# The middle low part of the convolution operands made on GpSimd instead of VectorE, in a fused decoder kernel on one Trainium2 core

## What is computed

```python
x = _layernorm(x + _L0_attn_ref(x, ...), axis=-1)      # 32 heads of 16, softmax attention, output projection wo
x = _layernorm(x + _L0_xattn_ref(x, ctx_1024, ...))    # width-2 causal convolution, gates, cell
x = _layernorm(x + _L0_ffn_ref(x, ...), axis=-1)       # x quantized to integers, ternary weight, bias
```

```python
conv = lax.conv_general_dilated(xp, weight, window_strides=(1,), padding='VALID', ...)
out = uss + conv + bias[None, :, None]
it, ot, gt, ft = jnp.split(out, 4, axis=1)
it, ot, gt, ft = (sigmoid(it), sigmoid(ot), jnp.tanh(gt), sigmoid(ft))
ct = ft * z0c + it * gt
ht = ot * jnp.tanh(ct)
```

## Time and profile before

| | |
|---|---|
| runs | 2153.88, 2157.04, 2160.73 us |
| profiled execution, its own time | 2158.94 us |
| span in the profile, first to last instruction | 2156.9 us |
| mean granted TensorE clock | 0.978 |
| PE busy | 2084.8 us, 97% |
| DVE busy | 1663.5 us, 77% |
| ACT busy | 1313.6 us, 61% |
| POOL busy | 492.8 us, 23% |
| pair 0: projection, convolution | from about 1701, from 1754.75 us |
| pair 1: projection, convolution | from about 1906, from about 1976 us |
| last convolution matmul, end | 2122, 2154.4 us |

### The profile page before, as it was taken

The page is one execution under the profiler, slowest core; times in us unless marked ns, Lnnn a source line. Parts: engine busy times, 40 slices in busy tenths (PEclk is TensorE's granted clock), DMA queues, the critical chain, the costliest instruction groups (busy, mean ns, idle before and its releaser), DMA issues. The chain is left out here.

```text
span 2156.9 us, 39825 instructions
## 1 busy us (share of the span) xinstructions
PE 2084.8 (97%) x11264; PEld 1174.6 (54%) x11264; DVE 1663.5 (77%) x1729; ACT 1313.6 (61%) x2429; POOL 492.8 (23%) x972
## 2 busy tenths in 40 slices
PE   9999999999999999999999999999999899988996
PEld 4788775444444444444444444444444477756773
DVE  4333356888999999999989999998998367885786
ACT  0112113778888888888888888888887533443344
POOL 0000000121212212121221212122121452564244
PEclk9999998999999999999999999999999999998997
DMA  4456645456475565665665564655657567744672
GB/s 161 137 156 157 179 127 98 80 117 135 101 135 130 101 139 112 112 138 97 132 137 101 126 136 101 135 128 103 138 110 207 166 251 302 281 172 137 234 259 79
DMA packets 205965, 315.24 MB, mean 146 GB/s; under 512 B 105168, under 2 KB 105168, under 8 KB 193616
## 3 DMA queue, kind: packets, MB, share of 16 engines
q1 hardware_dynamic: 205904, 314.47, 57.9%
HBM read 211.06 MB, written 101.19 MB: 145 GB/s over the span
## 5 line engine op out<-in xcount | busy, mean ns | idle before, releaser
L233 DVE TENSOR_REDUCE neg_max<-psum 128x1 f32<-128x1024 f32 x1024 | 1205.9, 1219 | 139.8 <-PE psum L226 139.7
L612 ACT ACTIVATE probs<-psum 128x512 f32<-128x512 f32 x2048 | 1065.3, 606 | 281.3 <-PE psum L539 277.0
L539 PE MATMUL psum<-q_op,k_op 50*128 50x512 f32 x2048 | 753.7, 452 | 8.1 <-POOLq L683 3.3
L539 PEld LDWEIGHTS psum<-q_op,k_op 50*128 50x128 f32 x2048 | 354.8, 192 | 586.5 <-ACT probs L612 566.3
L226 PE MATMUL psum<-k_op,q_op 48*128 48x512 f32 x2048 | 623.0, 480 | 0.8 <-DVE neg_max L233 0.8
L548 PE MATMUL psum<-probs,v_op 128*32 128x512 f32 x4096 | 549.8, 609 | 5.7 <-ACT probs L612 2.9
L226 PEld LDWEIGHTS psum<-k_op,q_op 48*128 48x128 f32 x2048 | 390.5, 315 | 20.7 <-issue 4.4
L191 PE MATMUL psum<-x_wino,conv_w 128*128 128x512 f32 x1152 | 275.2, 395 | 0.7 <-DMA conv_w<-conv_w_parts_dram 0.7
L191 PEld LDWEIGHTS psum<-x_wino,conv_w 128*128 128x128 f32 x1152 | 214.6, 188 | 46.7 <-issue 1.1
L244 POOL CAST neg_max_parts<-neg_max 128x8 fp32r<-128x8 f32 x128 | 24.5, 191 | 918.8 <-DVE neg_max L233 918.8
L548 PEld LDWEIGHTS psum<-probs,v_op 128*32 128x32 f32 x4096 | 82.6, 108 | 137.3 <-ACT probs L612 69.3
(11 more groups left out here) (104 smaller groups left out, 1665.5 us busy)
## 6 DMA issues: line engine op xcount, KB each, us to landing
q_op<-qk_parts_dram SPq DMA_DIRECT2D x384, 128.0 KB, 4.1
conv_w<-conv_w_parts_dram SPq DMA_DIRECT2D x32, 1536.0 KB, 6.7
qk_parts_dram<-qk_parts SPq DMA_DIRECT2D x128, 256.0 KB, 3.2
k_op<-qk_parts_dram SPq DMA_DIRECT2D x384, 64.0 KB, 4.1
conv_w_parts_dram<-conv_w_parts SPq DMA_DIRECT2D x16, 1536.0 KB, 6.1
attended_dram<-out SPq DMA_DIRECT2D x64, 256.0 KB, 2.2
attended_parts_dram<-o_parts SPq DMA_DIRECT2D x128, 128.0 KB, 2.3
gates<-in_ctx_dram SPq DMA_DIRECT2D x32, 512.0 KB, 7.6
```

The costliest lines, as they stand in the source:

```text
L233: nc.vector.tensor_reduce(ops["max"][b][:, t:t + 1], mem["pair"][t % 2][:], AX_X, ALU.max, negate=True).then_inc(ops["maxed"], 1)
L539: nc.tensor.matmul(score_bank(i, n, j, last), kop[i][r, j // 2, n // 2 * P:(n // 2 + 1) * P], qop[i][r, j // 2, j % 2 * HALF:(j % 2 + 1) * ...
L612: nc.scalar.activation(probs[n % DEEP][:, j, :], score_bank(k, n, j, last), ACT.Exp, scale=SCALE).then_inc(exp_done, 1)
```

## The change

`low_parts` on VectorE no longer makes the middle low part. A new function of GpSimd, `middle_low`, makes it at the same step of the stage (for the tile of step i - 2), behind `inv_std` of step i and ahead of `last_term` of step i - 1. It waits for the same count of `wx_hi` as VectorE did and counts a new semaphore, `wx_mid`. TensorE waits for `wx_mid` beside `wx_made` in slot 0. The short description that goes with the change also names FFN tiles 7 to 12, brought forward into the last four convolution slots of each pair; the diff, which is whole here, touches no FFN tile and none of the tables.

```diff
@@ -899,6 +899,7 @@
         wx_made = sem("x_wino_made")
+        wx_mid = sem("x_wino_mid_made")
         c_in = [sem(f"c_in{g}") for g in range(4)]
@@ -1102,6 +1103,13 @@
+                def middle_low(p, w):
+
+                    bi, c = wo_tile(w)
+                    pool.wait_ge(wx_hi, 3 * (2 * p * KC + w) + 1)
+                    G.tensor_tensor(wx[1][1][:, c, bi, :], x1[:, bi, c, 1:F + 1:2], wx[1][0][:, c, bi, :].bitcast(F32),
+                                    ALU.subtract).then_inc(wx_mid, 1)
+
                 def wo_stage(p):
@@ -1113,6 +1121,8 @@
                         inv_std("wo", p, pos)
+                        if wino_of(p, i - 2) is not None:
+                            middle_low(p, wino_of(p, i - 2))
                         if wino_of(p, i - 1) is not None:
                             last_term(p, wino_of(p, i - 1))
@@ -1280,6 +1290,7 @@
                     if s == 0:
                         pe.wait_ge(wx_made, 2 * p * KC + WO_TILES.index((1, c)) + 1)
+                        pe.wait_ge(wx_mid, 2 * p * KC + WO_TILES.index((1, c)) + 1)
@@ -1386,9 +1397,6 @@
                 def low_parts(p, w):
                     bi, c = wo_tile(w)
                     n = 2 * p * KC + w
-                    dve.wait_ge(wx_hi, 3 * n + 1)
-                    V.tensor_tensor(wx[1][1][:, c, bi, :], x1[:, bi, c, 1:F + 1:2], wx[1][0][:, c, bi, :].bitcast(F32),
-                                    ALU.subtract)
                     dve.wait_ge(wx_first, n + 1)
```

## The result

The changed kernel takes 2165.32 us in the median of 13 executions, the kernel before 2158.41 in the median of 13. The ratio is 1.0034, 95% interval 1.0021 to 1.0048: slower by 7.3 us (4.5 to 10.4). The forecast was 2158.9, range 2153.5 to 2163.5, "no change" at 0.89. It was wrong. One execution took 3532 us and is left out of the ratio.

What follows compares the result with a forecast made beforehand. VectorE and GpSimd were taken as full in pair 0's projection stage, hidden behind TensorE, with pair 1's chain exposed; 0.7 + 1.15 = 1.85 us, rounded 1.9, on 2157.04 gave 2158.9, range 2153.5 to 2163.5.

Steps and rivals of the forecast that it cites:

- pair 0's margin: Ahead of convolution slot 0 in pair 0: VectorE's `y` of position 12 could slip 2.5 us before TensorE waits.
- three instances on pair 1's chain: Pair 1's projection stage: three middle parts on GpSimd delay the chain, 3 x 0.57 = 1.7 us.
- rival (b): GpSimd's subtraction is dear, pair 0's margin breaks and the clock drops: 10.8 us slower, 2167.8; chance 0.06.
- signs of being wrong: GpSimd instances above 0.8 us, over 3 us gap ahead of slot 0 with 0.63 us matmuls, `wx_mid` wait, changed tail.
- price p: GpSimd's time for one middle part in either pair's projection stage, taken as 0.57 us from `last_term`.
- Pair 0's delay of VectorE: Pair 0's projection stage: six middle parts ahead of position 8's `inv_std` make VectorE 3.0 us later.
- The walk: Instruction-by-instruction estimate of both pairs' projection stages: 0.7 us later in pair 0, 1.15 us in pair 1.
- The 0.7: Ahead of convolution slot 0 in pair 0: TensorE stands still for 0.7 us.
- The clock: Matmuls behind the stall ahead of slot 0 run at 1.2 instead of 2.4 GHz, some 2.4 us more.
- Pair 1: 1.15 us forecast: Pair 1's projection stage: 0.85 us later `y` of position 7 plus 0.3 us for low parts beside GpSimd's bias addition.
- Rival (a): VectorE bound both projection stretches and GpSimd takes the work for nothing: -2.1 us, 2154.9; chance 0.22.
- Rival (c): FFN tiles 7 to 12 really brought forward, three tiles leaving the tail: 2149 at best; chance 0.03.

Runs made afterwards that it cites:

- both make it: Kernel before, VectorE unchanged, with GpSimd also writing the middle low parts into a spare tile nobody reads; ratio to before 1.0039.
- float32 copy: As both make it, but GpSimd's spare result is float32 instead of the reduced format; executed once, no ratio, end mark 463.1 us.
- swapped kernel: Changed kernel with GpSimd's `last_term` placed ahead of `middle_low`; ratio to before 1.0029.
- pair 0 only: Kernel before with `middle_low` on GpSimd for pair 0 alone, VectorE keeping the instruction in pair 1; ratio to before 1.0028.
- pair 1 only: Kernel before with `middle_low` on GpSimd for pair 1 alone, VectorE keeping the instruction in pair 0; ratio to before 1.0013.
- before with early additions: Kernel before, four GpSimd bias additions of pair 0 moved ahead of its last normalisation: 0.9996; a second version also rearranges pair 1's additions: 0.9985.
- changed again: The changed kernel repeated without edits; ratio to before 1.0028.
- before again: The kernel before, profiled once more without edits; no ratio, end mark 452.7 us.
- changed with early additions: Changed kernel, with four of GpSimd's bias additions in pair 0 moved ahead of its last normalisation; ratio to before 1.0028.

## Why the prediction was wrong, step by step

**Right.** Which stretches matter; that pair 0's margin would be used up; the three instances on pair 1's chain; that the wait on `wx_mid` plays no part (the first 41 matmuls of slot 0 run without a gap) and no FFN tile has moved; and, as rival (b) and among the signs of being wrong, a stall of over 3 us ahead of slot 0 with slow matmuls behind it.

**The price p.** Taken 0.57 us, measured 0.70 from start to start and 0.744 as recorded. `last_term` was the nearest row, and it was 0.13 us too cheap. The Trainium skill's ratio of 1.96 ("GPSIMD Engine Reference", "Elementwise — side-by-side cycle accounting"), which would give an estimated 0.77, was closer than the row; the trace agrees with it to 0.03. This isn't what made the forecast wrong: by the prediction's own sum, 0.70 gives 1.85 + 9 x 0.13 = 3.0 us, and the page's 0.77 gives 3.7.

**Pair 0's delay of VectorE: 3.0 us forecast, 4.2 measured** (steps of 35.7 against 31.6). The dearer middle parts make 3.8 of it, 3.0 + 6 x 0.13. The walk also took the low parts at their undisturbed length, and two of them take up to 1.5 us where they run beside GpSimd's bias addition.

**The margin of 2.5 us: the step that failed.** It was read from one execution, in which o_lo came late and the reciprocals early. The other two executions with pair 0's code as it was show 0.3 us and a wait of 0.22. So 4.2 us of delay cost TensorE about 4 us (3.27 to 4.39), not 0.7. (The 0.7 itself is 0.6 by its own terms, 3.0 + 0.14 - 2.54.)

**The clock.** Priced at 2.4 us, but only in rival (b), as it was thought to follow from a stall of over 3 us, and that to need p = 0.95. The stall was that long at p = 0.70. From the first convolution matmul to pair 1's first transposes it is 153.4, 153.3 and 153.4 us in the kernels with 3.90, 4.39 and 3.27 us of idle time, and 151.6 to 151.9 in those with none or little: 1.7 us. With 5.30 us, where both make it, it is 154.1, and with 4.57, in the float32 copy of it, 153.4. The length of the stall alone doesn't decide, though: the swapped kernel, with 3.31 us, has 152.0, and its granted clock stayed at 1.00 behind the stall, where it was 0.83 behind the 3.27 us of pair 0 only (stretch behind slot 0's start in the swapped kernel):

```profile
1758.70:1768.70 10.00, 9.99 (x44) 8.30 (x45) 6.69 (x13) 4.09 (x5) 6.44 (x22) 1.00 0.05 9
```

What decides isn't shown.

**Pair 0 together.** From the first projection matmul to pair 1's first transposes it is 204.1 us in the mean of the five profiles in which VectorE makes the part in pair 0 and GpSimd doesn't (before twice, pair 1 only, and the two of the kernel before with early additions), 210.3 in the mean of changed, changed again and pair 0 only: 6.2 us against 0.7. The swapped kernel is at 207.5; with it the difference is 5.5. Some of it is chance: GpSimd's last normalisation starts at 13.2 in the mean of the five and at 14.4 in that of the three, and the change touches no code that runs ahead of that mark.

**Pair 1: 1.15 us forecast.** From its first transposes to projection tile 13 it is 59.7, 59.9 and 59.2 us in before, before again and pair 0 only, and 62.4, 62.3 and 60.5 in changed, changed again and pair 1 only: 2.1 us in the mean. (The same code of pair 1 gave 58.4 in before with early additions and 60.9 in changed with early additions, so single profiles scatter by 1.5 to 2 us.) Three instances at 0.70 make 2.1; I had counted 0.85 of relief on VectorE's side. None shows in the sum, and VectorE idled 1.41 us ahead of `first_term`. Part of the difference is o_lo itself, 9.36 us against 8.00; why isn't shown.

**The sum** is 6.2 + 2.1 = 8.3 us, or 7.6 with the swapped kernel in pair 0's mean, against 7.3 and 6.0 timed. Rival (a), -2.1 us, falls by the result, and by the kernel in which nobody makes the part: without the work on either engine it is between 1.5 us faster and 4.3 slower. Rival (c) took its 2149 from the profiled execution; from the median that the forecast starts at it would be 2147.3. The form of rival (b) was right, and it got 0.06, for its price was set at 1.29 us a piece and its threshold at 0.95: with a margin of 0.3 us the same formula puts it at about 0.6.

## What to carry to other kernels

The margin between the two engines is a difference of two times that here each hang on a DMA; one profile gives one draw of it. Before a change is called hidden by such a margin, set it to zero once and see what the sum becomes: here that alone turns 1.9 us into over 4, and the clock follows. And an engine that is 23% busy over the span can be full in the one stage where work is to be put on it; relieving the other engine then brings little (0.7 us of 5.6 here). Where two engines' instructions lengthen each other, ask what each will run beside after the move, and not only how long it was before.

## What was not expected of the hardware

A 128x256 subtraction on GpSimd took 0.74 us with its operands in two tiles and 0.61 with both in one, and the type of the result made no difference (0.740 and 0.742). Two low parts on VectorE, 0.75 us by themselves, took up to 1.57 us in the changed kernel and 1.55 in the swapped one where they ran beside GpSimd's 128x512 bias addition. That GpSimd is busy isn't enough: before, it was busy 23.90 of 25.00 us and they took 0.75, since the middle part had the bias addition beside it. TensorE's granted clock, in the mean of the 10 us behind a stall, was 0.83 for one of 3.27 us (pair 0 only) and 1.00 for one of 3.31 (swapped).
